# Spreading delta over the state partitions by DMA instead of by matmul, in a four-layer convolution and state-space kernel on one Trainium2 core

## The reference

```python
u = silu(causal_conv(in_proj(xn)))            # 32 inner channels for each 16-channel chunk
delta = softplus(dt_proj(x_proj_dt(u)) + b)
def step(h, inputs):                          # over the 3136 tokens of an image
    d_t, u_t, B_t, C_t = inputs
    dA = exp(d_t[..., None] * A)              # 16 states for every inner channel
    h = h * dA + (d_t * u_t)[..., None] * B_t[:, None, :]
    y = einsum('gdn,gn->gd', h, C_t)
    return h, y
out = chunk + out_proj((y + u * D) * silu(z))
```

## Time and profile before

| | |
|---|---|
| median of 3 runs | 10410.15 us (10389.02 to 10415.18) |
| the profiled execution | 10411.98 us, span 10410.2 us, mean granted TensorE clock 0.878 |
| busy over the span | PE 80%, PEld 41%, DVE 73%, ACT 53%, POOL 52% |
| DMA over the span | 403 MB, mean 39 GB/s |

### The profile page before, as it was taken

One profiled execution on the slowest core, in us unless ns is written; L12 is line 12 of the kernel. 1 busy time (PEld: TensorE's weight loads), 2 busy tenths in 40 slices (PEclk: granted clock), 3 DMA queues, 4 the chain that ended last, 5 costly groups with the idle time before them and its releaser, 6 DMA issues. The chain is left out here.

```text
span 10410.2 us, 140735 instructions
## 1 busy us (share of the span) xinstructions
PE 8332.9 (80%) x34187; PEld 4314.8 (41%) x34187; DVE 7595.6 (73%) x10036; ACT 5478.6 (53%) x9098; POOL 5384.7 (52%) x4490
## 2 busy tenths in 40 slices
PE   9977777777777777777777777777777899999997
PEld 9942222222222222222222222222222599977996
DVE  7769898898989898898989889898988112211222
ACT  0346666666666666666666666666666013311332
POOL 0027677777777777676777777677777000000000
PEclk9978888878888888888888788888888999999998
DMA  9631111111111111111111111111111100030002
GB/s 175 170 80 33 32 35 30 38 28 35 32 32 35 29 36 28 38 29 35 33 31 36 28 36 31 33 32 32 35 30 36 56 10 0 0 75 19 0 0 49
DMA packets 644678, 403.37 MB, mean 39 GB/s; under 512 B 399312, under 2 KB 631120, under 8 KB 643664
## 3 DMA queue, kind: packets, MB, share of 16 engines
q1 hardware_dynamic: 407888, 318.19, 12.2%
q10 hardware_dynamic: 236032, 77.08, 3.2%
HBM read 136.43 MB, written 103.80 MB: 23 GB/s over the span
## 5 line engine op out<-in xcount | busy, mean ns | idle before, releaser
L636 POOL TENSOR_TENSOR prod<-hs,bsp 128x448 f32<-128x448 f32 x3584 | 4378.9, 1248 | 1489.7 <-PE ps L647 800.0
L624 DVE TENSOR_TENSOR_SCAN hs<-da,hs,ps 128x448 f32<-128x448 f32 x3072 | 3482.8, 1134 | 1.5
L605 ACT ACTIVATE da<-ps,nega 128x448 f32<-128x448 f32 x3586 | 2215.2, 634 | 1746.5 <-PE ps L588 1698.8
L597 PE MATMUL ps<-stack,seld 96*128 96x448 bf16 x3586 | 1438.1, 401 | 1643.0 <-DVE hs L624 1603.6
L615 DVE TENSOR_TENSOR ps<-ps,bsp 128x448 f32<-128x448 f32 x3585 | 2190.3, 611 | 658.3 <-PE ps L597 634.7
L597 PEld LDWEIGHTS ps<-stack,seld 96*128 96x128 bf16 x3586 | 357.7, 100 | 3442.7 <-DVE hs L624 2917.5
L887 PE MATMUL ps<-pv,ws 128*128 128x224 f32 x8800 | 1692.3, 354 | 9.4 <-ACT pv L1040 7.1
L887 PEld LDWEIGHTS ps<-pv,ws 128*128 128x128 f32 x8800 | 1656.8, 188 | 45.5 <-issue 7.8
L588 PE MATMUL ps<-stack,seld 96*128 96x448 bf16 x3587 | 1428.4, 398 | 177.3 <-ACT da L605 177.3
L1221 DVE SCALAR_TENSOR_TENSOR pv<-ps,R 128x224 f32<-128x224 f32 x880 | 422.1, 480 | 1279.4 <-PE ps L887 1279.4
L647 PE MATMUL ps<-prod,wc 128*32 128x448 f32 x7200 | 1039.0, 655 | 0.0
(11 more groups left out here) (120 smaller groups left out, 8203.5 us busy)
## 6 DMA issues: line engine op xcount, KB each, us to landing
stack<-parts SPq DMA_DIRECT2D x2700, 56.0 KB, 2.0
lnx<-in_x SPq DMA_DIRECT2D x118, 224.0 KB, 2.5
lny<-y_nchw SPq DMA_DIRECT2D x118, 224.0 KB, 2.7
x_column_pairs<-otile SPq DMA_DIRECT2D x225, 116.0 KB, 1.7
xpad<-x_column_pairs SPq DMA_DIRECT2D x32, 812.0 KB, 4.3
xpad<-in_x SPq DMA_DIRECT2D x64, 392.0 KB, 6.8
y_pairs<-yout ACTq DMA_DIRECT2D x32, 784.0 KB, 6.9
yin<-y_pairs SPq DMA_DIRECT2D x32, 784.0 KB, 4.3
```

The lines of the kernel that those rows point to most:

```text
L597: pe.matmul(ps[:, du_bank(st, j), 0:T], seld[0:96, b, :], stack[:, st.t % 2, 1, grp, :], start=True, stop=True).then_inc(S["du_spread"], 1)
L605: a.activation(da[:, j % 8, :], ps[:, D_BANK + j % 2, 0:T], ACT.Exp, scale=nega[:, j:j + 1])\
L624: v.tensor_tensor_scan(hs[:, j, :], da[:, j % 8, :], ps[:, du_bank(st, j), 0:T], 0.0 if first else hs[:, j, T - 1:T], ALU.mult, ALU.add)\
L636: g.tensor_tensor(prod[:, j % 8, :], hs[:, j, :], bsp[:, st.t % 2, 1, :], ALU.mult)\
```

## The change

delta is no longer cut into parts and spread by PE. SP writes each tile's delta to DRAM (copy_delta) and then, for each unit, reads its 8 rows back 16 times over into the unit's `da` slot (load_spread). ACT takes the exponential in place in SBUF. Only du is cast, stacked and spread, so parts, rest and stack are half as large. The PSUM banks of delta are free, and du has four banks. Its lead grows from 2 to 3, decay's from 2 to 4. SP gets slots and a table of its own: its loads and the 12 smaller DMAs of the parts share one queue. The tasks are placed in new slots. The constants are laid out in another order (states outermost on the partitions), and that part of the diff is left out below.

```diff
-PE_AT = {0: ["bc0", "last3"], 3: ["bc1"], 5: ["project", "lnc"], 8: ["sum0", "lnv"], 10: ["tap0", "tap2"],
-         12: ["tap1"], 13: ["tap3", "sum1", "z", "dt"], 14: ["sum2"]}
-ACT_AT = {1: ["bc0"], 2: ["relu"], 4: ["bc1"], 5: ["cast0"], 6: ["evacuate"], 7: ["cast1"], 8: ["lnc"], 11: ["lnv"],
-          12: ["shift"], 14: ["silu", "u", "z", "exp"], 15: ["dt"]}
-DVE_AT = {0: ["add_x"], 3: ["min", "gate"], 6: ["rest0"], 8: ["rest1"], 10: ["scale"]}
-POOL_AT = {0: ["delta_log", "delta_u"]}
-LEAD = {"du": 2, "delta": 3, "decay": 2, "drive": 1}
+PE_AT = {1: ["last3"], 2: ["bc0"], 3: ["bc1"], 5: ["project", "lnc"], 7: ["sum0", "lnv", "tap0"], 8: ["tap1"],
+         9: ["tap2", "tap3"], 10: ["z"], 11: ["sum1", "dt"], 14: ["sum2"]}
+ACT_AT = {5: ["bc0"], 6: ["bc1"], 7: ["relu"], 8: ["cast0"], 9: ["lnc"], 10: ["evacuate"], 11: ["lnv", "cast1"],
+          13: ["shift"], 14: ["silu", "u", "z", "exp"], 15: ["dt"]}
+DVE_AT = {2: ["min"], 3: ["add_x", "gate"], 6: ["rest0"], 8: ["rest1"], 9: ["scale"]}
+POOL_AT = {0: ["delta_log"], 2: ["delta_u"]}
+SP_AT = {5: ["copy"], 7: ["part0"], 9: ["part1"], 10: ["part2"], 11: ["store"]}
+LEAD = {"du": 3, "decay": 4, "drive": 1}
...
+    copies = nc.dram_tensor("delta_copy", (2, P, T), F32, kind="Internal").ap()
...
-            rest = sb(m, "rest", [P, 2, T])
-            parts = sb(m, "parts", [P, 2, 3, T], BF16)
-            stack = sb(m, "stack", [96, 2, 2, GR, T], BF16)
+            rest = sb(m, "rest", [P, T])
+            parts = sb(m, "parts", [P, 3, T], BF16)
+            stack = sb(m, "stack", [96, 2, GR, T], BF16)
...
         def delta_times_u(g, st):
             if not st.ahead:
+                g.wait_ge(S["dlt_stored"], st.next * 16)
                 g.wait_ge(S["split"], st.next)
-                g.wait_ge(S["delta_u"], st.next)
...
+        def stack_part(sp, st, part):
+            if not st.ahead and part == 0:
+                sp.wait_ge(S["du_spread"], (st.next - 1) * UN + 1)
+                sp.sem_inc(S["gates"], 1)
+            if part < 2:
+                sp.wait_ge(S["cast"], st.next * 2 + (part + 1))
+            else:
+                sp.wait_ge(S["split"], st.next + 1)
+            for grp in range(GR):
+                sp.dma_start(stack[DI * part:DI * (part + 1), st.par, grp, :],
+                             parts[DI * grp:DI * (grp + 1), part, :]).then_inc(S["stacked"], 16)
+
+        def copy_delta(sp, st):
+            sp.wait_ge(S["delta"], st.next + 1)
+            sp.dma_start(copies[st.par], dlt[:, 0, :]).then_inc(S["dlt_stored"], 16)
+
+        def load_spread(sp, st, j):
+            b, grp = j // GR, j % GR
+            if j == 0:
+                sp.wait_ge(S["dlt_stored"], st.tile * 16 + 16)
+                sp.sem_inc(S["gates"], 1)
+            sp.wait_ge(S["scan_done"], st.tile * UN + j + 1)
+            lo = DI * grp + 8 * b
+            src = copies[st.t % 2, lo:lo + 8].partition_broadcast(NS)
+            sp.dma_start(da[:, j % SLOTS, :], src).then_inc(spread_in[j % SLOTS], 16)
...
-        def spread_delta(pe, st, j):
...
         def spread_du(pe, st, j):
...
-            pe.wait_ge(S["scan_done"], st.tile * UN + (j + 9 - du_bank_back(st, j)))
-            pe.matmul(ps[:, du_bank(st, j), 0:T], seld[0:96, b, :], stack[:, st.t % 2, 1, grp, :],
+            pe.wait_ge(S["scan_done"], st.tile * UN + j + 5)
+            pe.matmul(ps[:, DU_BANK + j % 4, 0:T], seld[0:96, b, :], stack[:, st.t % 2, grp, :],
                       start=True, stop=True).then_inc(S["du_spread"], 1)

         def decay(a, st, j):
-            n = st.tile * UN + j
-            a.wait_ge(S["d_spread"], n + 2)
-            a.wait_ge(S["scan_done"], n + 1)
-            a.activation(da[:, j % 8, :], ps[:, D_BANK + j % 2, 0:T], ACT.Exp, scale=nega[:, j:j + 1])\
+            a.wait_ge(spread_in[j % SLOTS], st.tile * (UN // SLOTS * 16) + (j // SLOTS + 1) * 16)
+            a.activation(da[:, j % SLOTS, :], da[:, j % SLOTS, :], ACT.Exp, scale=nega[:, j:j + 1])\
                 .then_inc(S["exp_done"], 1)
...
             with sp.Fori(0, PAIRS) as p:
                 for t in range(ST):
...
                     if st.has_ln:
                         ln_load(sp, st)
-                    stack_parts(sp, st)
-                    store(sp, tile, par, img, k)
+                    for j in range(UN):
+                        load_spread(sp, *unit(st, j + SLOTS))
+                        for name in SP_AT.get(j, ()):
+                            if name == "copy":
+                                copy_delta(sp, st)
+                            elif name == "store":
+                                store(sp, tile, par, img, k)
+                            else:
+                                stack_part(sp, st, int(name[4:]))
...
-                        spread_delta(pe, *unit(st, j + LEAD["delta"]))
```

More of the change, by code:

```diff
@@ L187, in build @@
             "cast", "rest", "split", "stacked",
-            "bc_ready", "d_spread", "du_spread", "exp_done", "dbu_done", "scan_done", "prod_done",
+            "dlt_stored", "bc_ready", "du_spread", "exp_done", "dbu_done", "scan_done", "prod_done",
             "y_summed", "y_gated", "out_mm", "out_evac", "out_stored0", "out_stored1")}
+        spread_in = [sem(f"c_spread_in{i}") for i in range(SLOTS)]
         D = {n: sem("d_" + n) for n in (
@@ L327, in build @@
         assert TMP % 2 == 0
[L328 to L339, removed]
+        DU_BANK, TMP_BANK, Y_BANK, O_BANK = 0, 5, 7, 7
         class Step:
@@ L549, in cast_part @@
                     a.wait_ge(S["stacked"], st.next * 192)
-                src = dlt[:, :, :]
+                src = dlt[:, 1, :]
             else:
                 a.wait_ge(S["rest"], st.next + 1)
-                src = rest[:, :, :]
-            a.copy(parts[:, :, part, :], src).then_inc(S["cast"], 1)
+                src = rest[:, :]
+            a.copy(parts[:, part, :], src).then_inc(S["cast"], 1)
         def rest_of(v, st, part):
@@ L558, in rest_of @@
             if part == 0:
-                v.tensor_tensor(rest[:, :, :], dlt[:, :, :], parts[:, :, 0, :], ALU.subtract).then_inc(S["rest"], 1)
+                v.tensor_tensor(rest[:, :], dlt[:, 1, :], parts[:, 0, :], ALU.subtract).then_inc(S["rest"], 1)
             else:
[L561 to L566, removed]
+                v.tensor_tensor(parts[:, 2, :], rest[:, :], parts[:, 1, :], ALU.subtract).then_inc(S["split"], 1)
@@ L759, in _ @@
             st = Ahead(0)
-            stack_parts(sp, st)
+            copy_delta(sp, st)
+            for j in range(SLOTS):
+                load_spread(sp, Step(0, 0), j)
+            for part in range(3):
+                stack_part(sp, st, part)
             with sp.Fori(0, PAIRS) as p:
@@ L813, in _ @@
                 sum_states(pe, -1, b, UB[-1])
[L814 to L818, removed]
+            for j in range(LEAD["du"]):
+                spread_du(pe, Step(0, 0), j)
             with pe.Fori(0, PAIRS) as p:
@@ L967, in _ @@
                         act_task(a, st, name)
-                    for part in range(2):
-                        cast_part(a, st, part)
+            st = Ahead(0)
+            for part in range(2):
+                cast_part(a, st, part)
             for j in range(LEAD["decay"]):
@@ L1089, in _ @@
             v.sem_inc(S["prod_done"], 16)
-            for name in ("d_spread", "du_spread", "y_gated", "out_mm", "sz_ready", "out_evac"):
+            for name in ("du_spread", "y_gated", "out_mm", "sz_ready", "out_evac"):
                 v.sem_inc(S[name], 1)
@@ L1296, in lay_out @@
     cm = C // HC
[L1297 to L1302, removed]
+    by_group = lambda v: v.reshape((GR, 4, 2) + v.shape[1:])
+    conv_in, gate_in = (np.zeros((2, HC, cm, 2, GR, 4, HC, 2), np.float32) for _ in range(2))
+    out_w = np.zeros((GR, 4, HC, 2, HC, cm), np.float32)
+    bc = np.zeros((GR, 4, HC, 2, 2, NS, HC, 2), np.float32)
+    dtr = np.zeros((HC, 2, GR, 4, HC, 2), np.float32)
     xp = a["L1_conv_x_proj_w"]
@@ L1305, in lay_out @@
         for s in range(2):
-            conv_in[s, c, :, s, :, c, :] = by_group(ip[:DI]).transpose(2, 0, 1)
-            gate_in[s, c, :, s, :, c, :] = by_group(ip[DI:]).transpose(2, 0, 1)
-        out_w[:, c, :, c, :] = by_group(np.ascontiguousarray(a["L1_conv_out_proj_w"].T))
+            conv_in[s, c, :, s, :, :, c] = by_group(ip[:DI]).transpose(3, 0, 1, 2)
+            gate_in[s, c, :, s, :, :, c] = by_group(ip[DI:]).transpose(3, 0, 1, 2)
+        out_w[:, :, c, :, c, :] = by_group(np.ascontiguousarray(a["L1_conv_out_proj_w"].T))
         for i in range(2):
-            bc[:, c, :, i, c] = by_group(np.ascontiguousarray(xp[1 + NS * i:1 + NS * (i + 1)].T))[:, :, None, :]
-        dtr[c, 0, :, c] = by_group(xp[0])
-        dtr[c, 1, :, c] = by_group(a["L1_conv_dt_proj_w"][:, 0])
-    place = lambda v: np.broadcast_to(by_group(v)[:, None], (GR, HC, n8) + v.shape[1:]).reshape((P,) + v.shape[1:])
```

(10 more changed lines are left out.)

26 lines of the change are left out of this document (14 added, 12 removed).

## The result

The changed kernel takes 12267.69 us (median of 4 runs, 12265.3 to 12275.53) against 10412.67 us before: 1.179 times as long, with a 95% interval of 1.177 to 1.181. The direction was forecast, the size was not: 1855 us slower against 590, and outside the range of 10530 to 11500 us.

The account below looks back on a forecast made before the run. DVE was taken to bound the Mamba stage: 28.1 us of work plus 7.25 us of waits make 35.4 us a step against 32.8, 590 us more over 224 tiles, so 11000 us, range 10530 to 11500 us.

Parts of the forecast that it names:

- min: DVE slot 2: min waits for POOL's product and two delta_log operations after scan 0, 0.65 us a step.
- rest0: DVE slot 6: rest0 waits for ACT's cast0, behind decay(12) and so scan 4, 0.85 us a step.
- rest1: DVE slot 8: rest1 waits for ACT's cast1, behind decay(15) and sometimes lnv, mean 3.1 us a step.
- The median row is nearest: 2.7 us.: Landing time of a delta load, bounded from DMAs of the same size in the trace: 2.7 us.
- three chains: Waits of rest0, rest1 and drive(15) on DVE, each running through a load's landing, taken as 2.7 us.
- PE's lnv on squared (POOL and DVE need nothing of it at once): PE's lnv waiting on squared, listed among the added waits with cover, at no cost.
- min and add_x at their old durations: DVE's work a step: only L559 and L561 change, 1.33 us less, giving 28.1 us.
- Chain 4: drive(15) waits for its du matmul behind dt, u, decay(18) and load 18: 7.3 us, cover 4.64, wait 2.65.
- full speed: PE's clock for dt: kept at 2.4 GHz in the sum, since taps, z and sum1 run ahead.
- the 250 us set aside at the upper end: PE at half clock in dt's two passes and the du matmul: 250 us over the stage, in the range only.
- The fast one: Rival: early-landing loads don't hold ACT; 28.8 us a step, 9515 us; chance 0.15, partial gains included.
- The late-loads rival: Rival: loads land at 4.3 us from reading the same rows or sharing queues; 12070 us; chance 0.09.

Follow-up runs that it names:

- runs 1 and 2: Changed kernel with 16 slots for da instead of 8: 10564.03 us; changed kernel with every load in the loop waiting for one scan more: 13655.66 us.
- run 4: Changed kernel with each load reading all 128 rows of the copy once instead of 8 rows 16 times: 11879.58 us.
- Run 3: Changed kernel with the evacuation moved from ACT slot 10 to slot 8: 11922.48 us, ratio 1.147 to the kernel before.
- Run 9: Changed kernel (8 da slots) with min back in DVE slot 3 and both delta operations in POOL slot 0: 11891.09 us, ratio 1.143.
- run 8: Changed kernel with a second copy of each du matmul on PE, into free bank 4: 12258.58 us, ratio 1.179.
- run 7: Changed kernel with 16 da slots, evacuation in ACT slot 8, min in DVE slot 3, both delta operations in POOL slot 0: 9777.89 us, ratio 0.940.
- run 10: The kernel of run 7 with rest1 moved from DVE slot 8 to slot 9: 9883.10 us, ratio 0.951.

## Why the prediction was right and wrong

**What bounds the kernel: right.** DVE's order sets the stage, and the forecast that decays tied to a young scan would hold ACT's tasks, and through them DVE, is shown by runs 1 and 2: taking the tie away gives 1704 us back, tightening it by one scan costs 1388. The four places were named rightly: waits at L524, L552, L554 and ahead of drive(15), and none at the scans.

**The sizes: too small at all four.** A step, forecast and measured (waits over 224 tiles): min 0.65 and 0.73 us, rest0 0.85 and 1.23, rest1 3.1 and 4.8, drive 2.65 and 5.1. That is 7.25 and 11.9 us. On top DVE's work was 29.3 us, not 28.1. The step was 41.1 us (9138 over 222.5 tiles) instead of 35.4. So the forecast was 5.7 us a step short: in the stage, drive's wait is 2.45 of it, rest1's 1.65, DVE's own work 1.2 and the other two waits 0.4. The steps of the prediction that failed follow, with what single edits gave back. These amounts overlap, and some hold waits that were forecast, so they don't add up to the 1268 us that were missing:

- **"The median row is nearest: 2.7 us."** It was 3.3, and 2.6 for a plain source (run 4). The term was 0.6 us short in three chains, about 400 us of waits. Run 4 takes 0.7 us off and 495 us of waits with it, of which 388 reached the time. I named reads of the same rows as a rival with 4.3 us and a chance of 0.09; they did land later, but the packets took no longer.
- **"PE's lnv on squared (POOL and DVE need nothing of it at once)"**, listed among the covered waits. DVE did need it: cast1 stands behind ACT's lnv, that waits for PE's, which stands behind sum0, and sum0 waits for the evacuation that the change moved to a later slot (out_evac in sum_states). I had priced lnv at its two ACT instructions. Run 3 gives back 345 us by moving the evacuation alone. (The share of 8 of 14 steps in this term is 7 of 14: 3.0 us instead of 3.1, which makes the miss no smaller.)
- **min and add_x at their old durations.** I moved min to slot 2 and counted its wait, but not that POOL, freed from waiting for it, would multiply at the same time. DVE's work was 1.2 us a step more than summed, 0.94 of it min's and 0.2 add_x's (0.4 us in half of the steps). Run 9 gives back 377 us, of which 145 are the wait that was forecast in size.
- **Chain 4** was 9.3 us in the step shown against 7.3: load 18 1.1 us late instead of 0.65 (a stack DMA takes 0.59 us to issue, median of 2700, not 0.38: four in 2.46 us), the landing, and 2.38 us from u to drive instead of 1.36, of which 0.84 are dt's two matmuls at half clock (1.83 against 0.99 us). I had kept full speed. Here PE's clock (the column ahead of the last two) in stretches of that step:

```profile
4022.00:4024.00 2.00, 2.00 (x10) 0.47 (x11) 0.00 (x0) 0.14 (x1) 0.36 (x1) 0.68 0.31 110
...
4031.00:4033.00 2.00, 1.02 (x9) 0.22 (x8) 2.00 (x4) 1.16 (x2) 1.57 (x2) 1.00 0.19 52
4033.00:4035.00 2.00, 0.00 (x0) 0.00 (x0) 2.00 (x3) 0.12 (x2) 1.49 (x2) 0.63 0.48 156
4035.00:4037.00 2.00, 0.00 (x0) 0.00 (x0) 0.32 (x1) 1.97 (x3) 1.17 (x2) 0.50 0.38 65
4037.00:4039.00 2.00, 1.29 (x2) 0.65 (x3) 0.00 (x0) 1.98 (x3) 0.00 (x0) 0.50 0.80 234
```

PE worked almost without a pause from 4020.11 to 4027.86. Its clock was 0.50 at 4020 to 4022, rose at 4022 to 4024 and was 1.00, 2.4 GHz, from 4024 until 4033. PE's last matmul before dt ended at 4032.02. With PE idle in the wait for u the clock was 0.63 and then 0.50, 1.2 GHz, and it stayed at 0.50 in dt. The Trainium skill ("TensorE: Matmul & The Clock Gate", Part 1) gives the rule that a paused array runs slow. By that rule dt had to run slow here, and the trace agrees. Over the stage a dt matmul took 1.00 us in the mean, against 0.5 at full speed, so the 250 us set aside at the upper end belonged into the sum, as an estimate: no run isolates it. Putting PE work back elsewhere in the step gave no time (run 8).

**The rivals.** The fast one did not happen here, but run 7, at 9778 us, is not far from its 9515 once the order allows it, so its size was fair and its condition (a landing under 1.85 us) was not the only way there: in run 7 the landing was 4.2 us. The late-loads rival came nearest in time (12070 us), and that is luck: the landing was 3.3 us and not its 4.3, and accounts for about 400 of the 1268 us.

## What to carry to other kernels

When a producer is moved from an engine to a DMA that waits for a buffer, every task queued behind the consumer on its engine inherits the age of that buffer's last reader; with the landing in the path, give the buffer enough slots to break the tie before moving anything. For each task that a table moves, follow its semaphores through every engine's queue, also those that were covered before: moving one evacuation two slots earlier gave back 345 us through three engines (run 3). And look at which two engines will now run side by side, and which of them starts first, not only at who waits.

## What the runs showed of the hardware that was not expected

**DVE beside POOL.** DVE operations with both inputs in SBUF take up to 2.6 times as long when they start while a POOL instruction is already running. Min took 0.60 us while POOL waited for it and 1.54 us when it started beside POOL's products, as it did 224 times in the changed kernel; add_x took 0.66 and 1.06. How much longer follows from what is left of the POOL instruction that runs when DVE's starts (medians over the whole traces): for min 1.06 us were left, and it took 0.94 longer; for add_x 0.57 and 0.40; for L559 of the kernel before 0.62 and 0.50; for its L561 0.09 and nothing. So the DVE instruction waits for POOL's to end, less 0.1 to 0.2 us. Scale shows both sides. In the loop of the changed kernel it always started ahead of POOL's product and took 0.66 us; in the step shown, scale started at 4028.36, and POOL's product, started 0.17 us behind it, took 1.49 us instead of 1.14. In run 10 scale started behind POOL 82 times and took 1.55 us in the mean, and 0.67 without POOL. Drive and the scan, which read one input from PSUM, kept 0.61 and 1.13 us in every run, though POOL ran beside most of them. The Trainium skill ("SBUF — State Buffer", Who interferes with whom) says that a DVE instruction with two SBUF inputs contends with a GpSimd instruction that reads SBUF, and that one with a single SBUF input doesn't, outside of certain fast modes. The traces agree. L559 before fits: 1.59 us in the loop, beside POOL's products, and 1.09 us for the same shape ahead of the loop, at 699.88 of its timeline, when POOL was idle. The order of the tables decides it: freeing POOL from a wait lengthened the instruction it used to wait for, and moving min back in runs 7 and 9 moved part of the cost to rest0.

**A repeated source.** A load of 224 KB landed in 3.3 us when its 16 copies came from the same 8 DRAM rows and in 2.6 us from 128 different rows, with 0.52 and 0.32 us of it for the issue on SP. The packets themselves took no longer (run 4).

**Landing under load.** With 16 slots, and so loads free to go early, the median landing rose to 4.1 us and ACT's wait for loads still fell from 4076.7 to 1022.6 us. A later landing costs little when the load is issued that much ahead of its use; it isn't free, since ACT still waits those 1022.6 us.
